# A graph layer's node stage: POOL issues the stores of the result, ScalarE issues all loads of x

## The chip, the cores and the metric

The kernel runs on one core of one Trainium2 chip. The metric is device time in microseconds (us), the median of three runs. The core's engines run beside each other and meet at semaphores: PE multiplies matrices, ACT (ScalarE) and DVE (VectorE) work on rows of 128 partitions, POOL (GpSimd) adds and gathers, SP (SyncE) issues transfers. ACT, SP and POOL can issue DMA transfers; 16 DMA engines carry them.

## The reference

One layer of a graph network with attention over 25,000 edges and 50,000 nodes, 256 columns each, in float32:

```
h   = relu(layernorm(x))
msg = relu(h[src] + edge_attr)
p   = msg @ W_fc.T + b_fc
scores = p @ Q.T                                  # 4 heads
alpha  = softmax of scores over the edges with one dst
pooled[n, head] = sum of alpha * p over the edges with dst = n
gate   = softmax(mean of p over those edges @ Wg.T + bg)
out    = x + sigmoid(sum over heads of gate * pooled)
```

The edges come sorted by dst, and the low nodes have most of the edges.

## The kernel before, in words

An edge stage handles 196 tiles of 128 edges: POOL gathers rows of x (line 443), ACT and DVE normalize and add, PE transposes and multiplies (lines 735 and 745), and p stays in the on-chip memory, 64 of its tiles passing through DRAM. A middle part works out one weight for each edge: softmax and gate together, so that the sum over heads is one weighted sum of p.

The node stage (the change is here) takes 391 node tiles of 128 nodes in groups of four: 97 whole groups and a last one of two tiles and 80 rows. A group's sums lie in two banks of PSUM, and three such places take turns. Work on sums goes in 586 steps, each one edge tile times one node tile: DVE makes a 128x128 matrix with the weights in their places (`spread`, line 1248), PE multiplies it with p into the group's place (line 829, two instructions a step). For each group g ACT then waits until its steps are done (`stepped`, from a table read every three groups, line 600) and until its output slot is free (`stored`), takes the sigmoid into slot g mod 4 of `yout` (line 597, 128x1024), and clears the place in PSUM for the group three later (line 573). POOL adds x (line 478) from slot g mod 4 of `xin`, in place in `yout`, and signals `summed`. The last whole group and the rest are added by DVE (lines 1286 to 1292).

The transfers of a group are 512 KB each way. ACT issues the store of group g-1 behind the clear of group g, after waiting for `summed` of group g-1 (`store`, line 605), and behind it the load of x for group g+3 into the slot which that addition has read (`load_x`, line 552). For every fourth group (slot 0) POOL issues that load itself, behind its own addition and a wait for it (`add_four`, line 482). The order is written out by hand; each engine works through its list and stops at each wait. The first four loads are issued ahead of the node stage. POOL's loop runs over four groups a turn, with the addresses of its transfers in registers; the first turn and the last stand outside the loop.

Names: `sig_done` counts sigmoids, `summed` POOL's additions, `x_in` and `x_pool` landed loads by slot, `stored` landed stores by slot, `last_summed` DVE's additions at the end.

Of the kernel before, what the change touches and what calls it, by code (L numbers as in the profile page):

```python
# [27 lines left out]
P = 128  # L28
# [6 lines left out]
def gnn_layer(nc, x, src, dst, edge_attr, w_fc, b_fc, q_w, g_w, b_g, out):  # L35
    N, D = x.shape
# [39 lines left out]
    GROUP = 4  # L76
# [15 lines left out]
    FULL = N // (GROUP * P)  # L92
# [2 lines left out]
    XS, YS = 4, 4  # L95
    PERIOD = 12
    ROUNDS = FULL // PERIOD
    BY_POOL = (0,)
    assert FULL % 4 == 1 and (FULL - 1) % 4 in BY_POOL
    assert PERIOD % SLOTS == 0 and PERIOD % XS == 0 and LAST_WHOLE == 2 and N % P and FULL % PERIOD == 1  # L100

    scratch = nc.dram_tensor("p_spill", [SPILL // 4 * P, 4 * T], F32).ap()
# [2 lines left out]
    with ExitStack() as ctx:  # L105
# [3 lines left out]
        def sem(name):  # L109
            return ctx.enter_context(nc.semaphore(name))  # L110
# [179 lines left out]
        reloaded = [sem("reloaded0"), sem("reloaded1")]  # L290
        sig_done, summed, last_summed = sem("sig_done"), sem("summed"), sem("last_summed")
        x_in = [sem(f"x_in{k}") for k in range(XS)]
        x_pool = [sem(f"x_pool{k}") for k in range(XS)]
        stored = [sem(f"stored{k}") for k in range(YS)]

        def rows_of(t):
            return LAST if t == TILES - 1 else P
# [114 lines left out]
        @block.gpsimd  # L412
        def _(pool):
            pool.memset(ident[:, :], 0.0).then_inc(pool_step, 1)
            pool.wait_ge(pool_step, 1)
            pool.affine_select(out=ident[:, :], in_=ident[:, :], compare_op=ALU.not_equal, fill=1.0, base=0,
                               pattern=[[-1, P]], channel_multiplier=1).then_inc(const_set, 1)
            pool.memset(ones[:, :], 1.0).then_inc(const_set, 1)
            pool.iota(tile_i[:, :], pattern=[[P, BLK]], base=0, channel_multiplier=1).then_inc(const_set, 1)
            pool.memset(eps[:, :], LN_EPS).then_inc(const_set, 1)  # L420
            pool.memset(zero[:, :], 0.0).then_inc(const_set, 1)
            pool.iota(step_nj, pattern=[[1, HALF]], base=0, channel_multiplier=HALF).then_inc(const_set, 1)
            pool.iota(end_k, pattern=[[GROUP, 3]], base=GROUP + AHEAD, channel_multiplier=3 * GROUP).then_inc(const_set, 1)
            pool.iota(column[:, :], pattern=[[1, P]], base=0, channel_multiplier=0).then_inc(const_set, 1)
            pool.iota(count_i, pattern=[[1, COLS]], base=0, channel_multiplier=0).then_inc(const_set, 1)
            pool.memset(logits[:, TILES - 1:TP, :], 0.0).then_inc(const_set, 1)
            pool.wait_ge(tile_0_in, 16)

            for t in range(TILES):
                k = t % BODY  # L430
                if t == 1:
                    pool.wait_ge(first_in, 16)
                if t == FIRST:
                    pool.wait_ge(idx_ready, 1)
                if t == RING - TAIL:
                    pool.wait_ge(table_summed, PARTS + 3)
                if t >= BODY:
                    pool.wait_ge(gathered[k], 16 * (t // BODY))
                if t >= AHEAD_OF_PE:
                    pool.wait_ge(multiplied, t - AHEAD_OF_PE + 1)  # L440
                if t >= RING + BODY:
                    pool.wait_ge(ln_done, t - BODY + 1)
                pool.indirect_dma_start(out=x_row(t), out_offset=None, in_=x,  # L443
                                        in_offset=bass.IndirectOffsetOnAxis(ap=idx[0:rows_of(t), t:t + 1], axis=0),
                                        ).then_inc(gathered[k], 16)

            sums = tot[:, 0:H, :]
            pool.wait_ge(ends_ready, 2)
            pool.tensor_scalar(sums, sums, 1e-9, None, ALU.max).then_inc(sums_ready, 1)  # L449
            pool.wait_ge(mean_ready, 1)  # L450
            pool.wait_ge(sums_ready, 1)
            pool.tensor_tensor(tot[:, 4:6, :], pair(sums)[:, :, 0, :], pair(sums)[:, :, 1, :], ALU.mult).then_inc(sums_ready, 1)
            pool.wait_ge(sums_ready, 2)
            pool.tensor_tensor(tot[:, 6, :], tot[:, 4, :], tot[:, 5, :], ALU.mult).then_inc(sums_ready, 1)
            pool.wait_ge(rows_copied, PARTS + 2)
            pool.wait_ge(chain_turned, 2)
            for b in range(BLK):
                pool.tensor_scalar(sel_1[:, b, :], step_tile[:, :], tile_f[:, b:b + 1], None, ALU.is_equal
                                   ).then_inc(selected, 1)
            pool.wait_ge(gain_ready, 1)  # L460
            by_head = lambda a: a.rearrange("p h (b e) -> p h b e", b=BLK)
            gain_of = gain[:, :, 0, :].rearrange("p b h -> p h b").unsqueeze(3).broadcast_to([P, H, BLK, P])
            pool.tensor_tensor(by_head(sums), by_head(w_run), gain_of, ALU.mult).then_inc(by_first_done, 1)
            pool.wait_ge(by_first_done, 1)
            pool.tensor_tensor(tot[:, 0:2, :], tot[:, 0:2, :], tot[:, 2:4, :], ALU.add).then_inc(by_first_done, 1)
            pool.wait_ge(by_first_done, 2)
            pool.tensor_tensor(tot[:, 0, :], tot[:, 0, :], tot[:, 1, :], ALU.add).then_inc(by_first_done, 1)

            x_later = x[0:FULL * GROUP * P, :].rearrange("(t p) d -> p t d", p=P)

            def add_four(g0, first, more):
                for slot in range(4):
                    pool.wait_ge(sig_done, g0 + slot + 1)
                    if first or slot not in BY_POOL:
                        pool.wait_ge(x_in[slot], g0 * 4 + 16)
                    else:
                        pool.wait_ge(x_pool[slot], g0 * 4)
                    pool.tensor_tensor(yout[:, slot, :, :], yout[:, slot, :, :], xin[:, slot, :, :],  # L478
                                       ALU.add).then_inc(summed, 1)
                    if slot in more:  # L480
                        pool.wait_ge(summed, g0 + slot + 1)
                        pool.dma_start(xin[:, slot, :, :], x_later[:, bass.ds((g0 + slot + XS) * GROUP, GROUP), :]  # L482
                                       ).then_inc(x_pool[slot], 16)

            add_four(0, True, BY_POOL)
            with pool.Fori(1, FULL // 4 - 1) as four:
                add_four(four * 4, False, BY_POOL)
            add_four(FULL - FULL % 4 - 4, False, [k for k in BY_POOL if FULL - FULL % 4 + k < FULL])

        @block.scalar  # L490
        def _(act):
# [108 lines left out]
                word = act.value_load(done_of[:, bass.ds(three, 1)], min_val=0, max_val=(1 << 30) - 1)  # L600
                return word & 1023, (word >> 10) & 1023, word >> 20

            def store(g, slot):
                act.wait_ge(summed, g + 1)
                act.dma_start(o_rows[:, bass.ds(g * GROUP, GROUP), :], yout[:, slot, :, :]).then_inc(stored[slot], 16)  # L605

            def store_last_whole():
                act.wait_ge(last_summed, 1)
                act.dma_start(o_rows[:, (FULL - 1) * GROUP:FULL * GROUP, :], yout[:, (FULL - 1) % YS, :, :]
                              ).then_inc(stored[(FULL - 1) % YS], 16)  # L610

            for k in range(PERIOD):
                if k % 3 == 0:
# [3 lines left out]
                sigmoid(k, k, steps[k % 3])  # L617
                act.wait_ge(sig_done, k + 1)
                clear(k % SLOTS)
                if k:  # L620
                    store(k - 1, (k - 1) % YS)
                if k + 3 >= XS and (k + 3) % XS not in BY_POOL:
                    load_x(k + 3, (k + 3) % XS)
            with act.Fori(1, ROUNDS - 1) as r:
                for k in range(PERIOD):
# [4 lines left out]
                    sigmoid(g, k, steps[k % 3])  # L630
                    act.wait_ge(sig_done, g + 1)
                    clear(k % SLOTS)
                    store(g - 1, (k - 1) % YS)
                    if (k + 3) % XS not in BY_POOL:
                        load_x(g + 3, (k + 3) % XS)
            for g in range((ROUNDS - 1) * PERIOD, FULL):
                if g % 3 == 0:
                    steps = steps_of(g // 3)
# [2 lines left out]
                if g + SLOTS < GROUPS:  # L641
                    act.wait_ge(sig_done, g + 1)
                    clear(g % SLOTS)
                store(g - 1, (g - 1) % YS)
                if g + 3 < FULL and (g + 3) % XS not in BY_POOL:
                    load_x(g + 3, (g + 3) % XS)
                elif g + 3 == FULL:
                    load_last_x()
# [7 lines left out]
            store_last_whole()  # L656
            act.wait_ge(last_summed, 3)
            act.dma_start(out[FULL * GROUP * P:last_row, :].rearrange("(t p) d -> p t d", p=P),
                          yout[:, slot, 0:LAST_WHOLE, :]).then_inc(stored[slot], 16)
            act.dma_start(out[last_row:N, :], yout[0:N % P, slot, LAST_WHOLE, :]).then_inc(stored[slot], 16)  # L660
            for k in range(YS):
                act.wait_ge(stored[k], 16 * len(range(k, GROUPS, YS)) + (16 if k == slot else 0))


        @block.tensor
# [179 lines left out]
        def _(dve):  # L845
# [436 lines left out]

            slot = (FULL - 1) % 4
            dve.wait_ge(sig_done, FULL)
            dve.wait_ge(x_pool[slot], 16 * ((FULL - 1) // 4))
            v.tensor_tensor(yout[:, slot, :, :], yout[:, slot, :, :], xin[:, slot, :, :], ALU.add).then_inc(last_summed, 1)
            slot, left = FULL % 4, N % P
            dve.wait_ge(sig_done, FULL + 2)
# [30 lines left out]
```

## Time and profile before

| what | value |
|---|---|
| median of three runs | 654.74 us (654.54 to 656.39) |
| span of the profiled execution (first to last instruction) | 732.9 us |
| busy share of the span: PE, DVE, POOL, ACT | 75%, 67%, 62%, 52% |
| mean DMA throughput over the span | 234 GB/s |
| mean granted TensorE clock | 0.946 of full speed |

The page gives no other time of the profiled execution than its span; it is 78.1 us longer than the median of the timed runs. In the page a line like L478 is a line of the kernel. Engine names ending in q (ACTq, POOLq) are the issuing side of an engine. "Idle before" is the time in which the engine did nothing ahead of an instruction, with the event that ended it. The edge stage ends near 349 us, the middle part near 401, and the node stage fills the rest.

### The profile page before, as it was taken

How to read it: one execution, taken by the hardware profiler on the slowest of the kernel's cores; microseconds unless marked ns; L12 is line 12 of the kernel's file. 1: busy time of each engine (PE TensorE's matmuls, PEld its weight loads, DVE VectorE, ACT ScalarE, POOL GpSimd, SP SyncE). 2: the span in 40 equal slices, each digit the busy share in tenths (PEclk: the TensorE clock that was granted, in tenths of full speed). 3: DMA queues.
4: the chain of work that ended last, by engine and by line, in shares of the span. 5: the costliest groups of instructions: out<-in, count | busy, mean ns of one | idle time of the engine just before them, and what ended most of it. 6: DMA issues, size and time to landing. Idle time of an engine off the chain costs nothing.

```text
span 732.9 us, 12416 instructions
## 1 busy us (share of the span) xinstructions
PE 548.9 (75%) x2474; PEld 434.1 (59%) x2475; DVE 487.6 (67%) x1644; ACT 383.3 (52%) x661; POOL 453.4 (62%) x339
## 2 busy tenths in 40 slices
PE   2417988878779868879403998888888778877785
PEld 2205876666558656758202876776667566665564
DVE  4208678788879768769798766666565655555555
ACT  2105455656457545647211254666666666666674
POOL 7765565665560656550053366777877887778785
PEclk9999899999999999989855999999999999999999
DMA  7434455555553468775300799999999999999999
GB/s 223 131 93 134 147 173 174 165 174 154 174 170 114 129 224 271 237 234 191 115 0 1 247 355 383 314 307 329 357 319 329 325 327 339 325 337 336 341 333 332
DMA packets 137238, 171.53 MB, mean 234 GB/s; under 512 B 10096, under 2 KB 123784, under 8 KB 137202
## 3 DMA queue, kind: packets, MB, share of 16 engines
q10 hardware_dynamic: 91344, 90.23, 37.6%
q1 hardware_dynamic: 33010, 42.70, 18.6%
q0 software_dynamic: 12848, 38.20, 16.5%
q8 instruction: 12, 0.20, 0.1%
q14 instruction: 24, 0.20, 0.1%
HBM read 111.50 MB, written 59.60 MB: 233 GB/s over the span
## 4 chain that ended last, share of the span: by engine, by line
PE 52%; issue 12%; ACT 11%; DVE 10%; another core or an unknown queue 5%; ACTq 4%; DVEq 3%; POOL 2%; DMA 2%; POOLq 0%; SPq 0%
PE bank L745 24%; PE bank L829 18%; PE bank L735 7%; ACT arena L597 5%; DVE spread L1248 3%; ACT bank L573 3%; POOL arena L478 2%; ACTq L600 2%; DVEq L1252 1%; ACT arena L505 1%; ACTq L552 1%; ACTq L605 1%; ACT arena L497 1%; DMA p_keep<-p_spill 1%
## 5 line engine op out<-in xcount | busy, mean ns | idle before, releaser
L829 PE MATMUL bank<-p_keep,spread 128*128 x1172 | 274.1, 388 | 51.6 <-DVE spread L1248 46.7
L829 PEld LDWEIGHTS bank<-p_keep,spread 128*128 128x128 f32 x1172 | 219.0, 192 | 107.5 <-issue 79.8
L1248 DVE TENSOR_SCALAR spread<-bank,rel,wgt 128x128 f32<-128x128 f32 x586 | 195.8, 404 | 128.5 <-PE bank L829 72.8
L478 POOL TENSOR_TENSOR arena<-arena 128x1024 f32<-128x1024 f32 x96 | 224.9, 2352 | 73.1 <-ACT arena L597 72.7
L745 PE MATMUL bank<-w_all,arena 128*128 128x264 f32 (+1 forms) x784 | 228.0, 417 | 53.2 <-ACT arena L505 40.2
L745 PEld LDWEIGHTS bank<-w_all,arena 128*128 128x128 f32 (+1 forms) x784 | 143.7, 204 | 78.9 <-ACT arena L505 50.9
L597 ACT ACTIVATE arena<-bank 128x1024 f32<-128x1024 f32 x97 | 99.2, 1023 | 139.3 <-PE bank L829 120.3
L443 POOL DMA_INDIRECT p_keep<-in_x_dram,idx x124 | 120.8, 975 | 72.6 <-issue 31.5
L505 ACT ACTIVATE arena<-bank 128x256 f32<-128x256 f32 x196 | 73.6, 376 | 124.2 <-PE bank L735 71.0
L443 POOL DMA_INDIRECT arena<-in_x_dram,idx x72 | 70.1, 973 | 64.7 <-ACT arena L497 33.7
L573 ACT ACTIVATE bank<-zero 128x1024 f32<-128x1024 f32 x98 | 100.5, 1026 | 3.0
L735 PE MATMUL bank<-ident,arena 128*128 128x128 f32 x392 | 80.5, 289 | 24.4 <-DVE arena L1061 11.3
L735 PEld LDWEIGHTS bank<-ident,arena 128*128 128x128 f32 x392 | 56.8, 149 | 53.2 <-DVE arena L1061 13.5
L1061 DVE TENSOR_TENSOR arena<-arena 128x256 f32<-128x256 f32 x196 | 79.8, 408 | 6.7 <-issue 3.9
L497 ACT ACTIVATE arena<-p_keep,negmr,rstd 128x256 f32<-128x256 f32 x124 | 73.6, 594 | 20.3 <-issue 14.1
L1075 DVE TENSOR_TENSOR p_keep<-bank,bias 128x512 f32<-128x512 f32 x97 | 66.0, 680 | 0.0
L1073 DVE TENSOR_TENSOR logits<-bank,bias 128x16 f32<-128x16 f32 x97 | 16.5, 170 | 64.7 <-PE bank L745 34.6
L1055 DVE BATCH_NORM_STATS2 stats<-p_keep 128x6 f32<-128x256 f32 x124 | 51.7, 419 | 1.0 <-DMA p_keep<-in_x_dram,idx 0.6
L497 ACT ACTIVATE arena<-arena,negmr,rstd 128x256 f32<-128x256 f32 x72 | 42.7, 593 | 9.5 <-DVE negmr L1099 7.5
L1055 DVE BATCH_NORM_STATS2 stats<-arena 128x6 f32<-128x256 f32 x72 | 30.2, 419 | 0.0
L449 POOL TENSOR_SCALAR arena<-arena 128x1024 f32<-128x1024 f32 x1 | 3.9, 3852 | 42.5 <-DVEq L1183 42.5
L482 POOL DMA_DIRECT2D arena<-in_x_dram x24 | 18.6, 773 | 17.6 <-POOL arena L478 14.8
(202 smaller groups left out, 190.6 us busy)
## 6 DMA issues: line engine op xcount, KB each, us to landing
out_dram<-arena ACTq DMA_DIRECT2D x97, 512.0 KB, 4.5
arena<-in_x_dram ACTq DMA_DIRECT2D x73, 512.0 KB, 5.4
arena<-in_edge_attr_dram SPq DMA_DIRECT2D x48, 512.0 KB
arena<-in_x_dram POOLq DMA_DIRECT2D x24, 512.0 KB, 5.8
p_spill<-p_keep SPq DMA_DIRECT2D x16, 512.0 KB
p_keep<-p_spill SPq DMA_DIRECT2D x16, 512.0 KB, 5.8
p_keep<-in_x_dram,idx POOLq DMA_INDIRECT x124
arena<-in_x_dram,idx POOLq DMA_INDIRECT x72
```

The source lines that it names most:

```text
L443: pool.indirect_dma_start(out=x_row(t), out_offset=None, in_=x, in_offset=bass.IndirectOffsetOnAxis(ap=idx[0:rows_of(t), t:t + 1], axis=0) ...
L478: pool.tensor_tensor(yout[:, slot, :, :], yout[:, slot, :, :], xin[:, slot, :, :], ALU.add).then_inc(summed, 1)
L497: nc.scalar.activation(u[0:n, t % 4, :], x_row(t), ACT.Relu, bias=negmr[0:n, m:m + 1], scale=rstd[0:n, m:m + 1]).then_inc(ln_done, 1)
L505: nc.scalar.activation(msg_t[:, t % 4, :, 0:n], bank[:, TURNS_IN[t % len(TURNS_IN)], 0:D].rearrange("p (c e) -> p c e", c=KD)[:, :, 0:n], ...
L573: nc.scalar.activation(bank[:, 2 * z:2 * z + 2, :], zero[:, 0:1].unsqueeze(2).broadcast_to([P, 2, 512]), ACT.Copy).then_inc(zeroed, 1)
L597: nc.scalar.activation(yout[:, k % YS, :, :], places(k % SLOTS, GROUP), ACT.Sigmoid).then_inc(sig_done, 1)
L735: last = nc.tensor.transpose(bank[:, TURNS_IN[t % len(TURNS_IN)], c * P:c * P + n], u[0:n, t % 4, c * P:(c + 1) * P], ident[0:n, 0:n])
L745: last = nc.tensor.matmul(bank[0:n, 2 + t % 4, 0:NT], msg_t[:, t % 4, c, 0:n], w_all[:, c, :], start=(c == 0), stop=(c == KD - 1))
L829: nc.tensor.matmul(places[:, bass.ds(place, T)], spread[:, k0 + k, :], p_rows[:, bass.ds(p_at, T)], start=False, stop=True, skip_group_che ...
L1055: v.bn_stats(stats[0:n, m, :], x_row(t)).then_inc(stats_done, 1)
L1061: v.tensor_tensor(u[0:n, t % 4, :], u[0:n, t % 4, :], ea[0:n, t % BODY, :], ALU.add).then_inc(added, 1)
L1248: v.tensor_scalar(spread[:, k, :], bank[:, 7, P:2 * P], rel[:, bass.ds(s0 + k, 1)], wgt[:, bass.ds(s0 + k, 1)], ALU.is_equal, ALU.mult).th ...
```

## The change

POOL's loads of x go. Behind each of its 96 additions POOL now waits for `summed` and issues the store of that group itself. ACT issues no stores but those of the end (the last whole group and the rest), and issues the loads of x for all groups, each behind the wait for `summed` that stood ahead of the store. The stores of the end have a semaphore of their own, since `stored` is now signalled from POOL's queue. POOL's last turn goes into the loop.

```diff
-    BY_POOL = (0,)
-    assert FULL % 4 == 1 and (FULL - 1) % 4 in BY_POOL
+    assert FULL % 4 == 1
...
-        x_pool = [sem(f"x_pool{k}") for k in range(XS)]
-        stored = [sem(f"stored{k}") for k in range(YS)]
+        stored, last_stored = [sem(f"stored{k}") for k in range(YS)], sem("last_stored")
...
-            x_later = x[0:FULL * GROUP * P, :].rearrange("(t p) d -> p t d", p=P)
-
-            def add_four(g0, first, more):
+            y_rows = out[0:FULL * GROUP * P, :].rearrange("(t p) d -> p t d", p=P)
+
+            def add_four(g0):
                 for slot in range(4):
                     pool.wait_ge(sig_done, g0 + slot + 1)
-                    if first or slot not in BY_POOL:
-                        pool.wait_ge(x_in[slot], g0 * 4 + 16)
-                    else:
-                        pool.wait_ge(x_pool[slot], g0 * 4)
+                    pool.wait_ge(x_in[slot], g0 * 4 + 16)
                     pool.tensor_tensor(yout[:, slot, :, :], yout[:, slot, :, :], xin[:, slot, :, :],
                                        ALU.add).then_inc(summed, 1)
-                    if slot in more:
-                        pool.wait_ge(summed, g0 + slot + 1)
-                        pool.dma_start(xin[:, slot, :, :], x_later[:, bass.ds((g0 + slot + XS) * GROUP, GROUP), :]
-                                       ).then_inc(x_pool[slot], 16)
-
-            add_four(0, True, BY_POOL)
-            with pool.Fori(1, FULL // 4 - 1) as four:
-                add_four(four * 4, False, BY_POOL)
-            add_four(FULL - FULL % 4 - 4, False, [k for k in BY_POOL if FULL - FULL % 4 + k < FULL])
+                    pool.wait_ge(summed, g0 + slot + 1)
+                    pool.dma_start(y_rows[:, bass.ds((g0 + slot) * GROUP, GROUP), :], yout[:, slot, :, :]
+                                   ).then_inc(stored[slot], 16)
+
+            add_four(0)
+            with pool.Fori(1, FULL // 4) as four:
+                add_four(four * 4)
...
-            def store(g, slot):
-                act.wait_ge(summed, g + 1)
-                act.dma_start(o_rows[:, bass.ds(g * GROUP, GROUP), :], yout[:, slot, :, :]).then_inc(stored[slot], 16)
...
                     sigmoid(g, k, steps[k % 3])
                     act.wait_ge(sig_done, g + 1)
                     clear(k % SLOTS)
-                    store(g - 1, (k - 1) % YS)
-                    if (k + 3) % XS not in BY_POOL:
-                        load_x(g + 3, (k + 3) % XS)
+                    act.wait_ge(summed, g)
+                    load_x(g + 3, (k + 3) % XS)
...
             for k in range(YS):
-                act.wait_ge(stored[k], 16 * len(range(k, GROUPS, YS)) + (16 if k == slot else 0))
+                act.wait_ge(stored[k], 16 * len(range(k, FULL - 1, YS)))
+            act.wait_ge(last_stored, 48)
...
-            dve.wait_ge(x_pool[slot], 16 * ((FULL - 1) // 4))
+            dve.wait_ge(x_in[slot], 16 * ((FULL - 1) // 4) + 16)
```

POOL's list, in its loop over four groups of the node stage. `arena` holds both `xin` and `yout`, `out_dram` is the result. Before:

```order
L477 REGISTER_ALU
L478 TENSOR_TENSOR arena<-arena 128x1024
L482 ISA
L482 DMA arena<-in_x_dram 128x4x256
L473 REGISTER_ALU
L475 REGISTER_ALU
L478 TENSOR_TENSOR arena<-arena 128x1024
L473 REGISTER_ALU
L478 TENSOR_TENSOR arena<-arena 128x1024 x2
L486 REGISTER_ALU
L486 COMPARE_AND_BRANCH
```

After, one store behind each addition (line 473 is the addition now, 476 the store):

```order
L472 ISA
L473 TENSOR_TENSOR arena<-arena 128x1024
L476 ISA
L476 DMA out_dram<-arena 128x4x256
L471 REGISTER_ALU
L473 TENSOR_TENSOR arena<-arena 128x1024
L476 ISA
L476 DMA out_dram<-arena 128x4x256
L471 REGISTER_ALU
L473 TENSOR_TENSOR arena<-arena 128x1024
L476 ISA
L476 DMA out_dram<-arena 128x4x256
```

One load in four groups has become four stores, each with a register instruction ahead of it.

ACT's list in its loop, one group that has a load; ACTIVATE from `bank` is the sigmoid, ACTIVATE into `bank` the clear. Before:

```order
L596 REGISTER_ALU
L597 ACTIVATE arena<-bank 128x1024
L573 ACTIVATE bank<-zero 128x1024
L605 ISA
L605 DMA out_dram<-arena 128x4x256
L552 ISA
L552 DMA arena<-in_x_dram 128x4x256
```

After (line 590 the sigmoid, 566 the clear, 545 the load):

```order
L589 REGISTER_ALU
L590 ACTIVATE arena<-bank 128x1024
L566 ACTIVATE bank<-zero 128x1024
L545 ISA
L545 DMA arena<-in_x_dram 128x4x256
```

The store has gone from behind the clear, and the load stands there in every group.

## Rows read from the trace of the kernel before

**Rows 1.** Windows: us, busy PE, PEld, DVE, ACT, POOL, PE clock, DMA share, GB/s.
```profile
401.00:450.00 49.00, 45.55 (x205) 37.82 (x203) 34.95 (x105) 18.46 (x18) 23.02 (x12) 1.00 0.89 304
450.00:722.00 272.00, 223.94 (x948) 177.06 (x948) 158.11 (x474) 175.57 (x172) 216.40 (x108) 0.99 1.01 333
```

**Rows 2.** Waits, 412 to 725 us: waiter, releaser, us, times, longest.
```profile
ACT arena L597 <- PE bank L829: 120.3, 74, 23.9
...
POOL arena L478 <- ACT arena L597: 72.7, 57, 19.6
...
ACT arena L597 <- POOL arena L478: 16.4, 9, 3.3
POOL arena L482 <- POOL arena L478: 14.8, 23, 0.7
```

**Rows 3.** POOL's groups, 412 to 725 us: busy us, mean ns, idle before.
```profile
L478 POOL TENSOR_TENSOR arena<-arena 128x1024 f32<-128x1024 f32 x96 | 224.9, 2352 | 73.1 <-ACT arena L597 72.7
L482 POOL DMA_DIRECT2D arena<-in_x_dram x24 | 18.6, 773 | 17.6 <-POOL arena L478 14.8 <-issue 2.7
```

**Rows 4.** POOL in order of time: start, us, line, [idle before, releaser].
```profile
502.42 2.35 POOL L478 TENSOR_TENSOR arena<-arena 128x1024 f32<-128x1024 f32 x1 [1.53 <-ACT arena L597]
505.45 0.77 POOL L482 DMA_DIRECT2D arena<-in_x_dram  x1 [0.68 <-POOL arena L478]
506.24 4.66 POOL L478 TENSOR_TENSOR arena<-arena 128x1024 f32<-128x1024 f32 x2
```

**Rows 5.** POOL in order of time, the first ten groups.
```profile
412.22 2.35 POOL L478 TENSOR_TENSOR arena<-arena 128x1024 f32<-128x1024 f32 x1 [19.55 <-ACT arena L597]
414.87 0.86 POOL L482 DMA_DIRECT2D arena<-in_x_dram  x1 [0.30 <-POOL arena L478]
...
435.41 2.34 POOL L478 TENSOR_TENSOR arena<-arena 128x1024 f32<-128x1024 f32 x1 [1.49 <-ACT arena L597]
...
452.22 2.34 POOL L478 TENSOR_TENSOR arena<-arena 128x1024 f32<-128x1024 f32 x1 [1.68 <-ACT arena L597]
```

**Rows 6.** All engines in order of time, the end.
```profile
724.45 2.36 POOL L478 TENSOR_TENSOR arena<-arena 128x1024 f32<-128x1024 f32 x1 [0.76 <-ACT arena L597]
...
729.70 0.65 ACTq L660 DMA_DIRECT2D out_dram<-arena  x1
```

**Rows 7.** DMA view, 412 to 725 us: queues, then issues with us to landing.
```profile
q10 hardware_dynamic: 86188, 85.60, 83.3%
q0 software_dynamic: 3456, 12.58, 11.8%
...
out_dram<-arena ACTq DMA_DIRECT2D x95, 512.0 KB, 4.6
arena<-in_x_dram ACTq DMA_DIRECT2D x69, 512.0 KB, 5.4
arena<-in_x_dram POOLq DMA_DIRECT2D x24, 512.0 KB, 5.8
```

**Rows 8.** POOL's x loads, line 482: landing.
```profile
DMA to landing us min/median/max: 4.0/5.8/7.7
```

**Rows 9.** ScalarE (ACT) and its queue (ACTq) in order of time.
```profile
511.02 1.02 ACT L597 ACTIVATE arena<-bank 128x1024 f32<-128x1024 f32 x1 [3.33 <-POOL arena L478]
512.07 1.03 ACT L573 ACTIVATE bank<-zero 128x1024 f32<-128x1024 f32 x1
512.22 0.38 ACTq L605 DMA_DIRECT2D out_dram<-arena  x1
512.79 0.41 ACTq L552 DMA_DIRECT2D arena<-in_x_dram  x1
```

**Rows 10.** POOL's gathers, line 443: ns min/median/max, starts.
```profile
L443 POOL DMA_INDIRECT p_keep<-in_x_dram,idx x124: 951/957/1227, 4.2 to 195.8; - x124
```

**Rows 11.** ScalarE early in the edge stage.
```profile
57.97 0.38 ACT L505 ACTIVATE arena<-bank 128x256 f32<-128x256 f32 x1 [12.98 <-remote]
```

**Rows 12.** PE in order of time, one run of twelve instructions (six steps).
```profile
492.97 2.85 PE L829 MATMUL bank<-p_keep,spread 128*128 x12 [1.11 <-DVE spread L1248]
```

More of the change, by code:

```diff
@@ L609, in store_last_whole @@
                 act.dma_start(o_rows[:, (FULL - 1) * GROUP:FULL * GROUP, :], yout[:, (FULL - 1) % YS, :, :]
-                              ).then_inc(stored[(FULL - 1) % YS], 16)
+                              ).then_inc(last_stored, 16)
             for k in range(PERIOD):
@@ L619, in _ @@
                 clear(k % SLOTS)
-                if k:
-                    store(k - 1, (k - 1) % YS)
-                if k + 3 >= XS and (k + 3) % XS not in BY_POOL:
+                if k + 3 >= XS:
+                    act.wait_ge(summed, k)
                     load_x(k + 3, (k + 3) % XS)
@@ L643, in _ @@
                     clear(g % SLOTS)
-                store(g - 1, (g - 1) % YS)
-                if g + 3 < FULL and (g + 3) % XS not in BY_POOL:
+                act.wait_ge(summed, g)
+                if g + 3 < FULL:
                     load_x(g + 3, (g + 3) % XS)
@@ L658, in _ @@
             act.dma_start(out[FULL * GROUP * P:last_row, :].rearrange("(t p) d -> p t d", p=P),
-                          yout[:, slot, 0:LAST_WHOLE, :]).then_inc(stored[slot], 16)
-            act.dma_start(out[last_row:N, :], yout[0:N % P, slot, LAST_WHOLE, :]).then_inc(stored[slot], 16)
+                          yout[:, slot, 0:LAST_WHOLE, :]).then_inc(last_stored, 16)
+            act.dma_start(out[last_row:N, :], yout[0:N % P, slot, LAST_WHOLE, :]).then_inc(last_stored, 16)
             for k in range(YS):
-                act.wait_ge(stored[k], 16 * len(range(k, GROUPS, YS)) + (16 if k == slot else 0))
+                act.wait_ge(stored[k], 16 * len(range(k, FULL - 1, YS)))
+            act.wait_ge(last_stored, 48)
         @block.tensor
```

## The prediction, made before the changed kernel ran

> **What bounds the kernel now.** I read the windows of the stages first, then the waits of the node stage, then POOL's and ScalarE's instructions in order of time, and last the DMA view. The windows [rows 1] show the node stage, about 401 to 722 us, with nobody idle much: from 450 to 722 us PE works 224 of 272 us, POOL 216, ACT 176, and the 16 DMA engines' share is 1.01. The waits [rows 2] run both ways: ACT's sigmoid waits for PE (120.3 us in 74 pieces), POOL for ACT's sigmoid (72.7, the longest 19.6, which is the one before its first addition [rows 5]), and ACT for POOL 16.4 us in 9 pieces. So no engine alone holds the stage, but POOL is near to it: in the sums of the stage [rows 3] its 96 additions take 224.9 us, its 24 issues 18.6 and the idle time ahead of the issues 17.6; that is 261 of the 314.6 us from the start of its first addition to the end of its last [rows 5, 6].
>
> **What one issue costs POOL.** POOL's rows in order of time [rows 4] show an addition at 502.42 lasting 2.35 us, then 0.68 us idle until the issue at 505.45 (it waits for its own addition), then 0.77 us of issue, and the next addition starts at 506.24, 0.02 us after. Nothing of POOL's runs beside it. The cycle of an addition with an issue is thus 2.35 + 0.68 + 0.77 + 0.02 = 3.82 us; without an issue it is half of the 4.66 us that two additions in a row take, 2.33. The one issue of [rows 5], whose address stands fixed in the program where those of the loop come from a register, waited 0.30 us: with 0.77 of issue a cycle of 3.44 us.
>
> **The change, part by part.**
> POOL loses 24 x loads and gets 96 stores, one behind every addition, each with its wait for `summed`; 92 of them have register addresses (only the first four stand ahead of the loop). Today one group in four pays 1.46 us more than its addition; then all four do. That gives 3.82 us a group against the 3.17 us at which the groups now come from group 9 on ((724.45 - 452.22) / 86 [rows 5, 6]). POOL becomes the pace.
>
> How much: the first groups are held by their sigmoids, not by POOL. The addition of group 5 starts at 435.41; four cycles of 3.82 end at 450.69, before 452.22, where group 9 starts now, 1.68 us after the end of POOL's work before it [rows 5]. So up to group 9 nothing need be later. From there 86 more starts at 3.82 us each put the last addition at 452.22 + 328.5 = 780.7 and its end at 783.1 us. Now it ends at 724.45 + 2.36 = 726.8 [rows 6]. That is **+56.3 us**. What follows the last addition stays as it is: the sigmoid of the last rows, DVE's additions, the last store issue at 729.70 [rows 6] and the end at 732.9, 6.1 us in all. The last of POOL's stores is issued 1.45 us after that addition and lands within some 6 us more by the loads' times [rows 8], about the same moment: up to 1.5 us more, which I leave to the range.
>
> ACT loses 96 store issues (0.38 us each [rows 9]) and gets 24 loads (0.41 us). These run on its queue mostly beside its own clear (an issue at 512.22 lies inside the clear of 512.07), so I count nothing; were ACT the bound, it would give back at most 96 x 0.38 - 24 x 0.41 = 27 us, but only down to POOL's own pace. The wait for `summed` that stood ahead of the store now stands ahead of the load, at the same place in ACT's order, for the same addition. Behind it wait the next sigmoid and clear; ACT is one group ahead of POOL there, so POOL finds its sigmoid ready while it pays 1.45 us for the store.
>
> The loads: each is issued when addition g-1 is done and needed by addition g+3, four cycles (15.3 us) less one addition later, about 12.9 us; it lands in 5.4 us [rows 7]. Covered. The wait of the sigmoid for its output slot: a store must land before the sigmoid of four groups later. In a period of 4 x 3.82 = 15.28 us there go 2.35 + 0.68 + 1.02 (sigmoid [rows 9]) and about 0.1 of handing over, which leaves 11.1 us from issue to landing. POOL's loads of the same size land in 5.8 us, at most 7.7 [rows 8]. Covered, by these rows; a store by POOL is not in the trace.
>
> The bytes are unchanged. 37.7 MB net (72 transfers of 512 KB) go from q10 to q0. In the stage q10 spends 83.3% of 16 engines x 313 us on 85.6 MB (48.7 us per MB), q0 11.8% on 12.58 MB (47.0) [rows 7]: 1.7 x 37.7 / 16 = 4 us less for the engines together, and behind POOL's pace worth nothing.
>
> Bounds of the cycle: with the wait of the one fixed-address issue 3.44 us, so 452.22 + 86 x 3.44 + 2.35 = 750.4, +23.6 us; with no wait at all 3.14, where POOL would be done before today's end, 0. Upward, an issue as dear as a gather's (0.96 us [rows 10]) gives 4.01 us and +72.6. I take 3.82, the looped row with the same size and kind of address.
>
> **Profile and timed runs.** The page gives the profiled execution no time but its span, 732.9 us, 78.1 us more than the median of 654.74 (654.54 to 656.39). Where the timed runs save it the trace cannot say; a standstill of ACT early in the edge stage, 12.98 us [rows 11], looks like a candidate. What is saved in the node stage adds to my difference, since POOL's pace would not shrink with it. Its bounds: 0, and 43 us, since 586 steps of PE, two instructions each and twelve in 2.85 us, 0.475 us a step [rows 12], need 278 of the 321 us. The DMA share of 1.01 is the nearest row: transfers fill the stage, so little can go; I take 8 us. **654.74 + 56.3 + 8 = 719.0 us.**
>
> The DMA row shows all three issuers' packets filling the same engines. The Trainium skill, "DMA: Bandwidth & Descriptors", section "Issuing engines are not separate DMA queues", says that transfers from any engine run on the same 16 DMA engines, and that issuing from several saves only the sequencer's issue time, usually small beside the transfer. By that rule the move is worth nothing either way and the time stays 654.7 us. The rows of POOL [rows 4] speak against it: with its wait the issue costs POOL 1.45 us a group, where the group has 3.17.
>
> **Rivals.**
> 1. A cheaper issue: if the address is ready before the addition ends, the cycle is 3.44 us. For: the issue at 414.87 [rows 5]. Against: the 23 waits of POOL's issues for its own additions sum to 14.8 us [rows 2], 0.64 on average, which two of 0.30 and twenty-one of 0.68 make. Time: 654.74 + 23.6 + 8 = 686 us.
> 2. The store lands late, and the ring of four output slots becomes the pace. It decides above 11.1 us from issue to landing; at 14 us each group takes 0.72 us more, 86 groups 62 us: 781 us. Against: at most 7.7 us for loads, 4.6 for ACT's stores [rows 7, 8]. For: full DMA engines, and no store from this queue so far. The Trainium skill, same page, section "Anatomy of one DMA", puts this path at about 2.0 us plus bytes by 436 GB/s, an estimate of 3.2 us here; the trace has 4.0 at least [rows 8], so its rule is not this stage's.
> 3. No change: the issue hides, POOL's cycle stays under 3.17 us. It needs POOL's wait for its addition to vanish. 654.7 us. This is what the rule of the Trainium skill above would give.
> 4. Faster: as in 3, and the transfers decide, which then gain the 4 us above: 651 us. It decides only below a cycle of about 3.1 us, that is addition and issue alone. The rows of POOL exclude it unless a store's issue is half as dear as a load's.
> 5. The change not doing what it says: the order shows one store behind each addition and no load on POOL, so I give it nothing.
>
> **Chances.** Forecast 0.74 (its own range 696 to 750), cheaper issue 0.10, late landing 0.06, no change 0.05, faster 0.05. No change means within 0.3%, about 2 us, which is what a measurement can tell here. The range runs from 683 to 748, the lower end taking in most of the cheaper issue; outside stay rivals 2 to 4 and the forecast's edge, about 0.2. Faster 0.05, same 0.05, slower 0.90.
>
> **What would show it.** POOL busy and waiting for itself nearly without other waits from 452 us on, additions 3.82 us apart, each followed by 0.68 us idle and an issue of 0.77; POOL's waits for ACT down from 72.7 us to about 27 (19.6 before the first addition); ACT's sigmoids waiting for POOL instead of PE; DMA share in the stage down to about 0.85. Additions 3.4 us apart would mean rival 1; sigmoids waiting for landings of over 11 us, rival 2; POOL still waiting for ACT in most groups, rivals 3 or 4. A node stage longer by 56 in the profile but a timed difference far from it would refute only the 8 us.

## The result, and the profile after

The changed kernel takes 714.54 us (713.71 to 715.24, four runs) against 655.04 us of the kernel before (654.54 to 656.39, four runs of it): a ratio of 1.0871, 95% interval 1.082 to 1.0923. It is 59.5 us slower. Its profiled execution has a span of 712.4 us, 2 us under the median.

A window of the node stage after (columns as in [rows 1]), which here begins near 320 us:

```profile
380.00:640.00 260.00, 191.73 (x757) 149.78 (x755) 125.79 (x378) 138.79 (x136) 211.60 (x135) 0.91 0.82 275
```

The DMA share has fallen from 1.01 to 0.82, PE's busy share from 82% to 74% (191.73 of 260), and POOL's has risen to 81%, 212 of 260 us. PE's granted clock in this window is 0.91 of full speed, where [rows 1] had 0.99; but PE is idle more, not less, and the next rows show that POOL does not wait for what PE delivers, so the clock is not what holds the stage. The waits, the counterpart of [rows 2] (L590 is the sigmoid, L566 the clear, L1236 VectorE's matrix of weights, L817 PE's multiplication with it, L473 POOL's addition, L476 its store):

```profile
ACT arena L590 <- PE bank L817: 138.9, 62, 23.9
...
DVE spread L1236 <- ACT bank L566: 105.2, 38, 6.6
PE bank L817 <- DVE spread L1236: 87.4, 64, 5.7
...
POOL out_dram L476 <- POOL arena L473: 60.1, 92, 0.9
ACT arena L590 <- POOL arena L473: 35.5, 26, 2.4
POOL arena L473 <- ACT arena L590: 23.6, 4, 19.6
...
POOL out_dram L476 <- issue: 7.0, 4, 2.7
```

POOL's waits for the sigmoid are down to 23.6 us in 4 pieces, of which 19.6 lie before its first addition. What it waits for is itself, 60.1 us in 92 pieces ahead of its issues. POOL's groups, the counterpart of [rows 3]:

```profile
L473 POOL TENSOR_TENSOR arena<-arena 128x1024 f32<-128x1024 f32 x96 | 226.5, 2360 | 25.7 <-ACT arena L590 23.6
L476 POOL DMA_DIRECT2D out_dram<-arena x96 | 74.2, 772 | 67.1 <-POOL arena L473 60.1 <-issue 7.0
```

226.5 us of additions, 74.2 of issues and 67.1 of idle time ahead of them are 367.8 us; from the first addition to the end of the last go 372.4. POOL in order of time, the counterpart of [rows 4]:

```profile
406.13 2.37 POOL L473 TENSOR_TENSOR arena<-arena 128x1024 f32<-128x1024 f32 x1
409.16 0.77 POOL L476 DMA_DIRECT2D out_dram<-arena  x1 [0.66 <-POOL arena L473]
409.96 2.36 POOL L473 TENSOR_TENSOR arena<-arena 128x1024 f32<-128x1024 f32 x1
```

An addition of 2.37 us, 0.66 idle, an issue of 0.77, and the next addition 3.83 us after the one before it. The first groups, the counterpart of [rows 5]: the addition of group 4 starts at 350.65 and waits for nothing any more; from then on no addition waits for a sigmoid.

```profile
332.74 2.35 POOL L473 TENSOR_TENSOR arena<-arena 128x1024 f32<-128x1024 f32 x1 [19.56 <-ACT arena L590]
...
350.65 2.34 POOL L473 TENSOR_TENSOR arena<-arena 128x1024 f32<-128x1024 f32 x1
355.72 0.77 POOL L476 DMA_DIRECT2D out_dram<-arena  x1 [2.73 <-issue]
...
371.79 2.37 POOL L473 TENSOR_TENSOR arena<-arena 128x1024 f32<-128x1024 f32 x1
```

The end, the counterpart of [rows 6]: the last of POOL's additions, VectorE's addition of the last whole group (line 1274), and the last store issue.

```profile
702.81 2.35 POOL L473 TENSOR_TENSOR arena<-arena 128x1024 f32<-128x1024 f32 x1
703.06 3.19 DVE L1274 TENSOR_TENSOR arena<-arena 128x1024 f32<-128x1024 f32 x1 [4.90 <-ACT arena L590]
...
707.64 1.31 ACTq L647 DMA_DIRECT2D out_dram<-arena  x1
```

And the DMA view of 332 to 706 us with the landing of POOL's stores, the counterparts of [rows 7, 8]:

```profile
q10 hardware_dynamic: 49472, 49.11, 44.7%
q0 software_dynamic: 13680, 49.81, 33.7%
...
out_dram<-arena POOLq DMA_DIRECT2D x96, 512.0 KB, 4.8
arena<-in_x_dram ACTq DMA_DIRECT2D x93, 512.0 KB, 4.0
```

```profile
DMA to landing us min/median/max: 3.4/4.8/8.4
```

### The profile page after: what moved, and what is told of

Its sections match the earlier page's. It is cut to its first block, busy times and chain, and to the rows that moved or that the text cites. A ratio compares the mean times of both kernels' runs of the same rounds, so it can differ in the third digit from the quotient of the medians.

```text
span 712.4 us, 12492 instructions
## 1 busy us (share of the span) xinstructions
PE 551.8 (77%) x2474; PEld 431.8 (61%) x2475; DVE 485.4 (68%) x1644; ACT 381.7 (54%) x661; POOL 513.5 (72%) x411
## 4 chain that ended last, share of the span: by engine, by line
POOL 33%; DVE 24%; issue 21%; PE 13%; DMA 4%; POOLq 2%; ACT 1%; DVEq 0%; ACTq 0%; SPq 0%
POOL arena L473 31%; PE bank L733 7%; DVE arena L1049 5%; DVE p_keep L1063 5%; DVE stats L1043 4%; DMA arena<-in_x_dram,idx 3%; PE bank L817 3%; PE bank L723 2%; POOL p_keep L441 2%; DVE mv L1080 1%; POOLq L476 1%; POOL out_dram L476 1%; DVE logits L1061 1%; DMA p_keep<-in_x_dram,idx 1%; DVE arena L1163 1%
## 5 line engine op out<-in xcount | busy, mean ns | idle before, releaser
L817 PE MATMUL bank<-p_keep,spread 128*128 x1172 | 290.0, 404 | 89.1 <-DVE spread L1236 87.8
L817 PEld LDWEIGHTS bank<-p_keep,spread 128*128 128x128 f32 x1172 | 229.4, 201 | 149.9 <-issue 117.9
L1236 DVE TENSOR_SCALAR spread<-bank,rel,wgt 128x128 f32<-128x128 f32 x586 | 195.6, 403 | 182.6 <-ACT bank L566 105.2
L473 POOL TENSOR_TENSOR arena<-arena 128x1024 f32<-128x1024 f32 x96 | 226.5, 2360 | 25.7 <-ACT arena L590 23.6
L733 PE MATMUL bank<-w_all,arena 128*128 128x264 f32 (+1 forms) x784 | 215.4, 398 | 3.9 <-DVE p_keep L1063 3.4
L590 ACT ACTIVATE arena<-bank 128x1024 f32<-128x1024 f32 x97 | 99.4, 1024 | 195.3 <-PE bank L817 138.9
L733 PEld LDWEIGHTS bank<-w_all,arena 128*128 128x128 f32 (+1 forms) x784 | 135.3, 192 | 25.3 <-issue 7.5
L441 POOL DMA_INDIRECT p_keep<-in_x_dram,idx x124 | 122.7, 990 | 38.5 <-issue 32.0
L476 POOL DMA_DIRECT2D out_dram<-arena x96 | 74.2, 772 | 67.1 <-POOL arena L473 60.1
L566 ACT ACTIVATE bank<-zero 128x1024 f32<-128x1024 f32 x98 | 100.5, 1026 | 3.0
L498 ACT ACTIVATE arena<-bank 128x256 f32<-128x256 f32 x196 | 71.8, 367 | 10.5 <-PE bank L723 10.3
L723 PEld LDWEIGHTS bank<-ident,arena 128*128 128x128 f32 x392 | 51.6, 144 | 40.8 <-DVE arena L1049 19.7
L505 ACT ACTIVATE rstd<-mv,eps 128x4 f32<-128x4 f32 (+2 forms) x55 | 16.1, 295 | 21.6 <-DVE mv L1080 21.5
```

The source lines that it names most:

```text
L566: nc.scalar.activation(bank[:, 2 * z:2 * z + 2, :], zero[:, 0:1].unsqueeze(2).broadcast_to([P, 2, 512]), ACT.Copy).then_inc(zeroed, 1)
L590: nc.scalar.activation(yout[:, k % YS, :, :], places(k % SLOTS, GROUP), ACT.Sigmoid).then_inc(sig_done, 1)
L723: last = nc.tensor.transpose(bank[:, TURNS_IN[t % len(TURNS_IN)], c * P:c * P + n], u[0:n, t % 4, c * P:(c + 1) * P], ident[0:n, 0:n])
L733: last = nc.tensor.matmul(bank[0:n, 2 + t % 4, 0:NT], msg_t[:, t % 4, c, 0:n], w_all[:, c, :], start=(c == 0), stop=(c == KD - 1))
L817: nc.tensor.matmul(places[:, bass.ds(place, T)], spread[:, k0 + k, :], p_rows[:, bass.ds(p_at, T)], start=False, stop=True, skip_group_che ...
L1236: v.tensor_scalar(spread[:, k, :], bank[:, 7, P:2 * P], rel[:, bass.ds(s0 + k, 1)], wgt[:, bass.ds(s0 + k, 1)], ALU.is_equal, ALU.mult).th ...
```

## The experiments

All times are medians beside runs of the kernel before on the same chip; ratios are to that kernel, with their 95% interval. The experiments ran on three chips, so between two of them the ratios compare better than the medians. Each diff is to the changed kernel unless it says otherwise.

**The kernel before, profiled once more.** No edit.

> The kernel before, unchanged, profiled once more. Theory: the 78 us by which the first profile of it was longer than its timed runs lie ahead of the node stage (standstills of that one execution), so this span is about 653 us (median less about 1.7 us, as in the changed kernel), and from POOL's first addition (x+y) to the end of its last it takes 314 to 315 us as before. Rival: profiling stretches this kernel's node stage; then the span stays near 730 us, or the node stage comes out shorter than 314 us in a span near 653.

Measured: 657.37 us, one execution, with a span of 655.6 us. POOL's first and last addition in it:

```profile
333.40 2.35 POOL L478 TENSOR_TENSOR arena<-arena 128x1024 f32<-128x1024 f32 x1 [20.24 <-ACT arena L597]
...
647.06 2.35 POOL L478 TENSOR_TENSOR arena<-arena 128x1024 f32<-128x1024 f32 x1 [0.79 <-ACT arena L597]
```

From 333.40 to 649.41 are 316.0 us, against 314.6 in the first profile; there the first addition came at 412.22 [rows 5]. So the surplus of 78 us lay wholly ahead of the node stage, in one execution. The standstill of ACT [rows 11] has no counterpart here: between 21 and 62 us its longest wait is 4.63 us. What held that one execution up stays open. Its node stage is as long as in an execution that is as fast as the timed runs.

**Fixed addresses.**

```diff
-            add_four(0)
-            with pool.Fori(1, FULL // 4) as four:
-                add_four(four * 4)
+            for g0 in range(0, FULL - 1, 4):
+                add_four(g0)
```

> The changed kernel with POOL's loop written out, so that all 96 stores have fixed addresses. Theory A (of the 0.66 us between addition and issue, some 0.36 us is the address being computed and handed on after the wait): the wait falls to 0.30 us, POOL's cycle from 3.81 to 3.44 us, the time from 714.5 by 86 to 92 times 0.37 and the four 1.4 to 2.7 us gaps to 676 to 684 us. Rival B (0.66 us is the addition's own completion in the loop): cycle and time stay at 714 us.

Measured: 684.28 us, ratio 1.043 (1.0391 to 1.047). POOL in order of time (lines as in the changed kernel):

```profile
404.95 2.36 POOL L473 TENSOR_TENSOR arena<-arena 128x1024 f32<-128x1024 f32 x1
407.61 0.77 POOL L476 DMA_DIRECT2D out_dram<-arena  x1 [0.30 <-POOL arena L473]
408.40 2.37 POOL L473 TENSOR_TENSOR arena<-arena 128x1024 f32<-128x1024 f32 x1
```

The idle time is 0.30 us in place of 0.66, and the cycle 3.45 us. Theory A holds, with the time 0.3 us above its range: the larger part of the wait is not the addition's completion. 30 us of the loss go with it. It is the time and the cycle of rival 1, which needed an edit that the change does not have.

**The store one group late.**

```diff
+            def store(g, slot):
+                pool.wait_ge(summed, g + 1)
+                pool.dma_start(y_rows[:, bass.ds(g * GROUP, GROUP), :], yout[:, slot, :, :]
+                               ).then_inc(stored[slot], 16)
...
-                    pool.wait_ge(summed, g0 + slot + 1)
-                    pool.dma_start(y_rows[:, bass.ds((g0 + slot) * GROUP, GROUP), :], yout[:, slot, :, :]
-                                   ).then_inc(stored[slot], 16)
+                    if slot or not first:
+                        store(g0 + slot - 1, (slot - 1) % 4)
...
+            store(FULL - 2, (FULL - 2) % YS)
```

> The changed kernel with each store issued one group later: POOL adds group g, then stores group g-1, whose addition has long ended, so the wait for its own addition is gone; 96 stores on POOL as before. Theory A (POOL's cycle is the pace, made of 2.36 addition + 0.66 wait + 0.77 issue + 0.02): cycle 3.14 to 3.25 us, about the pace of the kernel before (3.17), so 654 to 662 us, POOL again waiting for ACT at times. Rival B (the gap ahead of an issue belongs to every issue on POOL, not to the wait): 3.5 to 3.8 us, 685 to 714 us. Rival C (stores issued by POOL cost elsewhere, by late landing or the DMA engines): over 690 us with POOL idle.

Measured: 666.65 us, ratio 1.0158 (1.0119 to 1.0198), 5 us over the expected range. POOL in order of time (L478 the addition, L471 the store):

```profile
569.74 2.35 POOL L478 TENSOR_TENSOR arena<-arena 128x1024 f32<-128x1024 f32 x1
572.02 0.77 POOL L471 DMA_DIRECT2D out_dram<-arena  x1
572.81 2.36 POOL L478 TENSOR_TENSOR arena<-arena 128x1024 f32<-128x1024 f32 x1
```

The issue follows the addition without a gap and the cycle is 3.07 us: 96 issues are still there, and 48 of the 59.5 us are gone. What is left shows in the waits (L595 is the sigmoid):

```profile
ACT arena L595 <- PE bank L822: 103.6, 55, 25.0
...
POOL arena L478 <- ACT arena L595: 47.5, 34, 21.6
ACT arena L595 <- DMA out_dram<-arena: 43.0, 25, 3.2
```

Sigmoids wait 43.0 us in 25 pieces for stores to land, which none did in the changed kernel: the output slot now comes free a group later. I had not counted that.

**The same with six output slots.** `YS` from 4 to 6, and POOL's loop over twelve groups.

```diff
-    XS, YS = 4, 4
+    XS, YS = 4, 6
```

> The store one group late, as before, with six output slots in place of four. In the run with four slots sigmoids waited 43 us for landings of stores, since the slot comes free a group later. Theory (with the wait for the own addition gone, the ring of slots was what remained): those waits go, POOL's cycle is 3.10 us, and the time falls from 666.7 to 650 to 657 us. Rival (the DMA engines, whose share is 0.99 or more in that stage, set it): the waits move elsewhere, 663 to 668 us.

Measured: 654.93 us, ratio 0.9963 (0.9932 to 0.9994). The longest wait of the sigmoid (L595):

```profile
ACT arena L595 <- PE bank L822: 138.3, 92, 25.4
```

The waits for landings are gone, the time is in the theory's range, and it is that of the kernel before, with 96 stores issued by POOL. So with six slots, and without the wait, neither the stores nor POOL's queue cost anything that this run can show. The kernel before was not run with six slots.

**The changed kernel with six output slots.** The same edits to `YS` and to POOL's loop, the store behind its own addition.

> The changed kernel with six output slots in place of four and nothing else. Theory (POOL's own cycle of 3.81 us is the pace, no landing is waited for): 710 to 715 us, the gaps at the loop's turns a little fewer. Rival (the ring of output slots holds POOL's cycle up): clearly under 700 us.

Measured: 715.12 us, ratio 1.0869 (1.0792 to 1.0946), at the upper end of the theory's range. In the changed kernel the slots do not matter; rival 2 of the prediction falls.

**Half the stores on POOL.**

```diff
+    POOL_STORES = (1, 3)
...
+                    if slot in POOL_STORES:
...
                     act.wait_ge(summed, g)
+                    if (k - 1) % YS not in POOL_STORES:
+                        store(g - 1, (k - 1) % YS)
                     load_x(g + 3, (k + 3) % XS)
```

> The changed kernel with the stores shared: POOL stores the groups of slots 1 and 3 behind their additions, ACT those of slots 0 and 2, ahead of its load; ACT loads all x. Theory A (only POOL's own pace made the change slow): two groups take POOL 3.81 + 2.36 = 6.17 us, 3.09 a group, under 3.17, so 652 to 660 us. Rival: a cost that goes with the number of POOL's stores, whatever its pace: half the loss stays, about 685 us.

Measured: 656.09 us, ratio 0.9989 (0.9961 to 1.0018). POOL in order of time (L474 the addition, L478 the store):

```profile
430.19 0.77 POOL L478 DMA_DIRECT2D out_dram<-arena  x1 [0.67 <-POOL arena L474]
430.98 4.67 POOL L474 TENSOR_TENSOR arena<-arena 128x1024 f32<-128x1024 f32 x2
436.30 0.77 POOL L478 DMA_DIRECT2D out_dram<-arena  x1 [0.66 <-POOL arena L474]
```

From one issue to the next, two groups later, go 6.11 us, 3.06 a group, under the 3.17 at which the rest of the kernel delivers. Half of the issues cost nothing that the run can show: the loss starts where POOL's cycle passes the pace of the others, and is not a price per store.

**POOL issues nothing; ACT issues everything.** As above with `POOL_STORES = ()`.

> POOL issues nothing in the node stage, it only adds; ACT issues all 96 stores and all loads of x, each behind the wait for the addition. It tells what ACT's issuing costs, the other half of the change. Theory (ACT's issues lie beside its own work, POOL at 2.36 us a group is far from the pace): 650 to 658 us. Rival (ACT's issuing is on the path, so taking the stores from it was worth something that POOL's pace then hid): 24 more issues of 0.4 us on ACT, 662 to 668 us.

Measured: 654.06 us, ratio 0.9944 (0.9904 to 0.9984), in the theory's range; the rival's 662 to 668 us did not come. The window of 450 to 640 us (columns as in [rows 1]):

```profile
450.00:640.00 190.00, 152.82 (x650) 119.41 (x651) 109.06 (x327) 125.53 (x123) 143.61 (x63) 1.00 1.03 338
```

**SP issues the stores.** ACT the first 11, SP those of groups 11 to 95 behind its reloads, POOL none.

```diff
+            def store_y(g, slot):
+                sp.wait_ge(summed, g + 1)
+                sp.dma_start(y_rows[:, bass.ds(g * GROUP, GROUP), :], yout[:, slot, :, :]).then_inc(stored[slot], 16)
```

> Stores moved off both: SP, idle after its reloads, issues the stores of groups 11 to 95, each behind the wait for its addition; ACT issues the first 11 stores and all loads, POOL only adds. The change's half for ACT without its half for POOL. Theory (the loss was POOL's alone, and ACT's issues are hidden): 648 to 658 us, no more than 1% below the kernel before. Rival (freeing ACT of the stores is worth up to 96 x 0.38 = 36 us once POOL doesn't take it back): 620 to 645 us.

Measured: 660.01 us, ratio 1.0024 (0.9983 to 1.0065). The same window:

```profile
450.00:640.00 190.00, 150.75 (x625) 120.09 (x624) 103.44 (x310) 120.69 (x118) 137.97 (x59) 0.96 0.98 326
```

The ratio is within the theory's; the median itself is 2 us over its range. With about 193 issues on ACT or about 108, with POOL at 2.36 us a group, the time stays within 1% of the kernel before. So ACT's half of the change is worth nothing that these runs can show, and the rival's gain of up to 36 us did not come. What SP's own issuing may cost is not told apart here.

**A quarter of the loads, POOL issuing nothing.** To the kernel with `POOL_STORES = ()`:

```diff
-            def load_x(g, slot):
-                act.dma_start(xin[:, slot, :, :], x_rows[:, bass.ds(g * GROUP, GROUP), :]).then_inc(x_in[slot], 16)
+            def load_x(g, slot, n=1):
+                act.dma_start(xin[:, slot, 0:n, :], x_rows[:, bass.ds(g * GROUP, n), :]).then_inc(x_in[slot], 16)
...
-                load_x(g, g)
+                load_x(g, g, GROUP)
```

> The kernel in which POOL issues nothing, with the loads of x behind the first four groups cut to one of four node tiles (128 KB in place of 512; three quarters of the output rows get an old x, so part of the computation is left out). 36 MB of some 105 MB of the node stage's transfers go. Theory (what is left as the pace at 654 us, with POOL at 2.36 us a group, is the DMA engines, whose share is 1.03 there): the stage shortens until PE's 278 us or the ring of clears hold it, 615 to 635 us. Rival (the ring of sigmoid, clear, VectorE and PE holds the pace, and the transfers only fill the time): 648 to 658 us.

Measured: 641.3 us, ratio 0.9785 (0.9726 to 0.9844). The same window:

```profile
450.00:640.00 190.00, 151.34 (x633) 118.63 (x632) 107.28 (x316) 123.87 (x122) 140.51 (x60) 0.97 0.69 216
```

Neither theory holds: the DMA share falls from 1.03 to 0.69, but the time only by 10 us (by the ratios) to 13 us (by the medians), which lies between the two ranges. That is what the cut transfers had cost the node stage. Behind them stands a second pace hardly faster, with PE busy 151 of 190 us where it was 153. Which part of the ring sets it was not tried.

**A quarter of the loads in the changed kernel.** The same edit.

> The same cut of the loads in the changed kernel (part of the computation is left out in the same way). Theory (POOL's cycle of 3.81 us is the pace and no transfer is): 711 to 715 us as with full loads, POOL's additions still 3.81 us apart, the DMA share near 0.55. Rival (transfers or their landing have a part in it): clearly under 705 us.

Measured: 713.67 us, ratio 1.0892 (1.0828 to 1.0956). POOL in order of time:

```profile
472.40 2.36 POOL L473 TENSOR_TENSOR arena<-arena 128x1024 f32<-128x1024 f32 x1
475.42 0.77 POOL L476 DMA_DIRECT2D out_dram<-arena  x1 [0.66 <-POOL arena L473]
476.21 2.36 POOL L473 TENSOR_TENSOR arena<-arena 128x1024 f32<-128x1024 f32 x1
```

The cycle is 3.81 us with the load traffic cut, and the time that of the changed kernel, in the theory's range. The loads have no part in its pace; that the stores' landing has none was shown by the run with six slots.

No version that computes the whole result beats the kernel before by more than 0.6%; the best, with all issues on ACT, is 654.06 us.

## Why the prediction was right

**POOL's cycle.** Predicted 3.82 us: 2.35 addition, 0.68 wait, 0.77 issue, 0.02. Measured 3.81 to 3.83: 2.36, 0.66, 0.77, 0.02. The looped load of the same size was the right row for the store. The wait was then taken away in two steps: without 0.36 us of it the cycle is 3.45 and the time 684 us, with no wait 3.07 and 667 us, and 655 us once the slots are enough.

**POOL becomes the pace.** Shown by what does not matter (slots, loads) and by the run with half the stores, where POOL at 3.06 us a group loses nothing.

**The sum of the stage.** Predicted +56.3 us. From the start of the first addition to the end of the last, the stage takes 372.4 us against 314.6, +57.8 (against the 316.0 of the second profile of the kernel before +56.4, so what follows is about as large as the difference between two executions). Its parts: group 9 comes 39.05 us after the first addition where I had 40.0 (-0.95); 86 starts from there take 331.0 us where I had 328.5 (+2.5). Longer gaps ahead of some issues, 1.42 us in place of 0.66 three times and about 0.87 four times, make 3.1 us of it, and a cycle of 3.81 in place of 3.82 takes some back.

The end is 1.2 us longer: from the end of POOL's last addition to the end of the span 7.2 us (705.16 to 712.4) in place of 6.1. The prediction had left up to 1.5 us of it to the range, for POOL's last store. Before, the end had VectorE's addition of the last whole group and the last transfer of 80 KB (the last number is us from issue to landing):

```profile
725.99 1.91 DVE L1286 TENSOR_TENSOR arena<-arena 128x1024 f32<-128x1024 f32 x1 [2.19 <-ACT arena L597]
...
out_dram<-arena ACTq DMA_DIRECT2D x1, 80.0 KB, 2.7
```

After, from 704 us on:

```profile
out_dram<-arena POOLq DMA_DIRECT2D x1, 512.0 KB, 3.7
...
out_dram<-arena ACTq DMA_DIRECT2D x1, 80.0 KB, 4.2
```

VectorE's addition, though longer (3.19 us), ends 1.09 us behind POOL's last in both kernels, and the last store is even issued a little earlier, 2.48 us behind it in place of 2.89. What takes longer is that store's transfer, 4.2 us from issue to landing in place of 2.7. POOL's own last store, issued at 705.81, lands before it. Whether its 512 KB, now among the last transfers, hold that store up was not tried.

**The 8 us for profile and timed runs.** Wrong in size: the term is 0. I read 78 us of difference as something that profiling might add in the node stage too and took 8 of a possible 43; the second profile shows that one execution had lost them ahead of the stage. Without the 8 us the forecast was 711.0, and the 714.54 measured are 3.5 us more: 1.5 of the stage, 1.2 of the end, and 0.8 that no row accounts for. The 8 us too much covered these 3.5 and left the forecast of 719.0 4.5 us too high; that the two errors had opposite signs is luck.

**What was counted as hidden.** ACT's 96 issues less: worth nothing, as said, and nothing that the runs can show without POOL's pace over them either. The loads are covered: 4.0 us to landing where 12.9 are free. The stores land in 4.8 us, at most 8.4, under the 11.1 worked out; when the store was moved a group later, in its own experiment, that margin was used up and sigmoids waited 43.0 us for landings. The DMA share came to 0.82 (forecast about 0.85), POOL's waits for ACT to 23.6 (about 27).

**A sign that was off.** I had ACT's sigmoids waiting for POOL instead of PE. They wait 35.5 us for POOL and still 138.9 for PE. PE in turn waits for VectorE (87.4 us), and VectorE for ACT's clears (105.2 us). In the kernel before, over its node stage, these were less:

```profile
DVE spread L1248 <- ACT bank L573: 49.9, 27, 4.5
PE bank L829 <- DVE spread L1248: 46.7, 50, 2.7
```

ACT comes to its clears no faster than POOL's `summed` lets it, so the waits fit PE being late because POOL is, and the wait naming the last link and not the first. This is argued from the waits; no run shows it by itself.

**The rule that spoke against it.** The rows of POOL decide: on this queue the issue with its wait costs 1.45 us of the engine that also adds, where the group had 3.17. On ACT and SP the issues lie beside other work: with 85 stores on SP in place of ACT the ratio to the kernel before is 1.0024 in place of 0.9944. The rule of the Trainium skill, "DMA: Bandwidth & Descriptors", section "Issuing engines are not separate DMA queues", fits ACT and SP here; it does not give the 59.5 us by which POOL's issues made this kernel slower.

## What to carry to other kernels

Give each engine a cycle: what it does for one unit of work, with its issues and the waits ahead of them, and compare it with the pace at which units come. Work added under that pace was free here (48 stores on POOL cost nothing that could be measured), work over it cost its full excess times the number of units (0.65 us x 86). An issue that waits for the instruction just before it on the same engine pays for the wait too; issuing it one unit later takes that away, if there are slots for it.

## What the runs showed of the hardware

**The address behind the wait.** An issue on POOL with a register address waits 0.66 us behind its addition, one with a fixed address 0.30 us. In the changed kernel the first four stores of all have 0.30 and those of the loop 0.66. With six slots, where twelve stores stand ahead of the loop, eleven of them have 0.30 or 0.31 and those of the loop 0.66 to 0.69; with the loop written out 88 of 96 have 0.30 or 0.31. The exceptions are those of the next paragraph. For each of the 92 stores with a register address the trace has two more instructions, the last at 705.2 and 705.3 us, right behind the end of the addition at 705.16:

```profile
L476 POOLq FUSED_REGOPS  x92: 37/48/51, 353.0 to 705.2; - x92
L476 POOLq MOVE out_dram<-arena x92: 29/29/38, 353.1 to 705.3; - x92
```

Register addresses and the loop come together in all these runs, so whether the loop has a part of its own is not shown.

**Longer gaps ahead of some issues.** In the changed kernel the 5th store waited 2.73 us, the 28th to 31st 0.85 to 0.90 us, and the 32nd, 60th and 88th 1.42 us, 28 apart:

```profile
564.02 2.36 POOL L473 TENSOR_TENSOR arena<-arena 128x1024 f32<-128x1024 f32 x1
567.80 0.77 POOL L476 DMA_DIRECT2D out_dram<-arena  x1 [1.42 <-issue]
```

With fixed addresses the same issues had the long gaps (2.34, 0.48 to 0.54 and 1.06 us). With half as many stores, so at other times and groups, it was again the 5th and the 32nd issue (2.71 and 1.47 us). But in the changed kernel with six slots, whose loop is three times as long, they were the 32nd, 58th and 84th, 26 apart:

```profile
560.38 0.77 POOL L476 DMA_DIRECT2D out_dram<-arena  x1 [1.37 <-issue]
```

So it is not a fixed number of issues alone. Where the store is issued one group late, only the 5th has a gap left, of 0.28 us. The cause was not tried.

**VectorE nearly stands while POOL adds.** VectorE's addition of the last whole group took 3.19 us in the changed kernel, where POOL's last addition ran beside it for 2.10 us; in the second profile of the kernel before it took 1.60 us, with 0.52 us beside POOL's (until 649.41); and with the store one group late 1.23 us, with POOL's addition over before it began:

```profile
648.89 1.60 DVE L1286 TENSOR_TENSOR arena<-arena 128x1024 f32<-128x1024 f32 x1 [2.53 <-ACT arena L597]
...
656.67 1.23 DVE L1279 TENSOR_TENSOR arena<-arena 128x1024 f32<-128x1024 f32 x1 [4.51 <-ACT arena L595]
```

Less the overlap the first two are 1.09 and 1.08 us. So whether the overlap was 0.52 or 2.10 us long, VectorE got only some 0.14 us of its work done in it. It fits the Trainium skill, "GPSIMD Engine Reference", section "Key points", which has the two engines contend where VectorE reads two inputs from the on-chip memory.
